# A GNN layer in one pipeline: x + beta split over two engines, two output tiles normalised by ScalarE, and the end transposes moved between the update halves

## The chip, the cores and the metric

The kernel runs on one core of a Trainium2 chip. A time is device microseconds of one execution. Its engines work side by side, each through its own instruction list in order, and meet at semaphores: TensorE (PE; its weight loads, which overlap the matmuls, are PEld), VectorE (DVE), ScalarE (ACT), GpSimd (POOL) and SyncE (SP), which here only issues DMAs.

## The reference

With 50,000 nodes of 128 features and 25,000 edges sorted by destination:

```python
h = relu(layernorm(x))                                    # no gamma, beta
e = [h[src], h[dst], edge_attr, node_vec[src], node_vec[dst]]
messages = silu(e @ mW1 + mb1) @ mW2 + mb2
agg = segment_sum(messages, dst)
u = silu([h, agg, node_vec] @ uW1 + ub1)
out = x + layernorm(h + u @ uW2 + ub2) * gamma + beta
```

All of it is float32.

## The kernel before, in words

Work is cut into 49 edge steps of 512 edges (4 tiles of 128) and 49 node steps of 1,024 nodes (8 tiles of 128). One software pipeline runs over iterations; each engine has a function `body(it)` that issues its part of iteration `it`. Iteration n handles edge step n (`new`: gathers and statistics), n-1 (`own`: normalise and transpose the gathered ends), n-2 (`e`: message network), and node steps n-3 (`nxt`), n-4 (`near`), n-5 (`k`), n-6 (`prev`). There are 56 iterations; edges end first, so the last ones are nodes alone. A first iteration is written out, then the sortedness of the edges is checked; the path used here is `WHOLE`.

What each engine does in an iteration, in order:

- **GpSimd** issues 8 indirect DMAs that gather the end rows of `new` (L373), then adds beta to the whole x tile of `near` (`x_beta`, L393, 1,024 columns).
- **TensorE**: (a) node hidden layer of `k`, L445 and L447, in which a 0/1 matrix `match` sums the messages of each node; (b) edge hidden layer of `e`, L456 to L458; (c) 8 transposes of `x_norm` of `near` into the PSUM tensor `ps_t`, L464; (d) edge output of `e`, L469; (e) the node update of `k` into `ps_upd`, 8 tiles in two halves of four, L476 and L477; each half waits until VectorE has read the same half of the step before (`centred_ready`); (f) 8 transposes of `ends_norm` of `own` into the same `ps_t`, L486, and 4 of edge features, L490. (f) waits for ScalarE's `ends_norm`. The next iteration's (a) stands behind (f).
- **ScalarE**: (1) copies `ps_t` and `ps_f` of `e` out, L537 and L538; (2) normalises 8 tiles into `x_norm`, L532; (3) silu into `hidden_n`, L549; (4) silu into `hidden_e`, L553; (5) copies the transposed x out of `ps_t` as `h_t`, L557, which waits for (c) on TensorE; (6) normalises 8 tiles into `ends_norm`, L532.
- **VectorE**: `bn_stats` of 8 tiles of `ps_upd` of `prev` (L677), 8 of x (L681), 8 of the gathered ends (L685, L686); copies the destination index (L652); then a chain of small operations on [128, 24] values that makes 1/sqrt(var) by an integer guess, a Halley and a Newton step (L702 to L743), with the eight `centred` operations (L632, `(ps_upd - mean) * gamma`) put between its links, and the message eviction (L643), `place` (L661) and `match` (L670) behind them. `rstd` and `minus` (= -mean * rstd) end the chain; then 8 operations `y_out = centred * rstd + x_beta` (L749).
- **SyncE** issues loads and stores in ring buffers of four (x, ends) or two (output, `match`).

```python
for j in range(N_TILES):
    if j % E_TILES == 0:
        wait(pe, centred_ready, 2 * k.n - 1 + j // E_TILES)
```

The order within each engine's list is written by hand; there is no planner.

## Time and profile before

| | us |
|---|---|
| median of three runs | 720.5 (715.4 to 722.17) |
| the profiled execution's own time | 722.67 |
| its span, first to last instruction | 720.8 |
| busy: TensorE / VectorE / ScalarE / GpSimd | 630.0 / 642.1 / 516.5 / 541.0 |
| mean granted TensorE clock, share of full | 0.974 |

The busy times are sums over the whole span, each of one engine; two engines near 90% do not say which of them sets the pace, since a wait of one for the other can run in a ring. A timeline row gives start, length and, in brackets, how long the engine had been idle before it and what it had waited for.

### The profile page before, as it was taken

The numbers are of one execution on the slowest core, as the hardware profiler recorded it, in microseconds if no ns is written. First come the engines' busy times: TensorE is split into PE (matmuls) and PEld (weight loads), VectorE is DVE, ScalarE is ACT, GpSimd is POOL, SyncE is SP. The second block draws the span as 40 slices with busy tenths as digits, with TensorE's granted clock in tenths as the row PEclk, the third lists the DMA queues.
The fourth block names the chain that finished last, engine by engine and source line by source line (L and its number), as shares of the span: only waits on it lengthen the run. The fifth ranks groups of instructions, "written<-read, shape, count | busy, mean of one in ns | idle before, by whom it ended". The sixth has DMA issues, their size and how long they took to land.

```text
span 720.8 us, 17511 instructions
## 1 busy us (share of the span) xinstructions
PE 630.0 (87%) x3830; PEld 466.2 (65%) x3830; DVE 642.1 (89%) x3060; ACT 516.5 (72%) x1034; POOL 541.0 (75%) x448
## 2 busy tenths in 40 slices
PE   1468999999999999999998998998998998999981
PEld 0235676766776776766766766766767767767771
DVE  4365699999999999999999999999999999999897
ACT  1546778778877787787787787787788788788630
POOL 7778878888888888888888888888888888881210
PEclk9966999999999999999999999999999999999997
DMA  6445556666666666666765766756666766765231
GB/s 133 111 115 131 151 164 160 186 187 163 180 186 163 190 179 163 189 181 161 194 177 160 204 169 166 202 163 170 199 160 179 196 156 180 198 161 173 87 122 69
DMA packets 119053, 118.54 MB, mean 164 GB/s; under 512 B 48764, under 2 KB 93615, under 8 KB 119010
## 3 DMA queue, kind: packets, MB, share of 16 engines
q1 hardware_dynamic: 104884, 91.41, 43.6%
q0 software_dynamic: 12608, 26.25, 16.4%
q10 hardware_dynamic: 1518, 0.42, 0.3%
q8 instruction: 13, 0.21, 0.1%
q14 instruction: 30, 0.25, 0.1%
HBM read 79.31 MB, written 38.70 MB: 164 GB/s over the span
## 4 chain that ended last, share of the span: by engine, by line
POOL 60%; issue 21%; PE 8%; DVE 6%; ACT 2%; DMA 1%; POOLq 1%; ACTq 0%
POOL ends_in L373 47%; POOL x_beta L393 13%; ACT ends_norm L532 2%; DVE y_out L749 1%; DVE centred L632 1%; PE ps_e L458 1%; PE ps_t L486 1%; PE ps_hid L445 1%; PE ps_hid L447 1%; PE ps_e L457 1%; PE ps_e L456 1%; DVE stats L677 1%; PE ps_t L464 1%; DMA ends_in<-in_rows,end_idx 1%; PE ps_f L490 0%
## 5 line engine op out<-in xcount | busy, mean ns | idle before, releaser
L373 POOL DMA_INDIRECT ends_in<-in_rows,end_idx x392 | 422.6, 1078 | 113.3 <-issue 112.5
L476 PE MATMUL ps_upd<-w_out,hidden_n 128*128 128x128 f32 x784 | 140.4, 284 | 33.6 <-DVE centred L632 31.6
L532 ACT ACTIVATE ends_norm<-ends_in,minus,rstd 128x128 f32<-128x128 f32 x392 | 155.9, 484 | 6.6 <-DVE minus L743 6.6
L532 ACT ACTIVATE x_norm<-x_in,minus,rstd 128x128 f32<-128x128 f32 x392 | 156.0, 488 | 6.3 <-DVE minus L743 6.3
L476 PEld LDWEIGHTS ps_upd<-w_out,hidden_n 128*128 128x128 f32 x784 | 119.4, 192 | 41.9 <-DVE centred L632 26.4
L393 POOL TENSOR_TENSOR x_beta<-x_in,beta_row 128x1024 f32<-128x1024 f32 x49 | 116.0, 2368 | 39.1 <-DVE y_out L749 38.2
L632 DVE SCALAR_TENSOR_TENSOR centred<-ps_upd,y_mean,gamma_row 128x128 f32<-128x128 f32 x392 | 135.0, 347 | 0.1
L447 PEld LDWEIGHTS ps_hid<-match,msg_in 113*128 113x128 f32 x784 | 103.0, 191 | 47.2 <-issue 47.2
L537 ACT ACTIVATE ends_t<-ps_t 128x1024 f32<-128x1024 f32 x49 | 50.2, 1024 | 90.9 <-PE ps_f L490 89.3
L477 PE MATMUL ps_upd<-const_sb,h_t 128*128 128x128 f32 x392 | 107.6, 274 | 0.0
L749 DVE SCALAR_TENSOR_TENSOR y_out<-centred,rstd,x_beta 128x128 f32<-128x128 f32 x392 | 107.1, 348 | 0.0
L447 PE MATMUL ps_hid<-match,msg_in 113*128 113x128 f32 x784 | 103.4, 275 | 0.0
L445 PE MATMUL ps_hid<-h_t,w_node 128*128 128x512 f32 x196 | 100.8, 596 | 0.1
L685 DVE BATCH_NORM_STATS2 stats<-ends_in 128x6 f32<-128x128 f32 x196 | 55.5, 283 | 48.6 <-DMA ends_in<-in_rows,end_idx 48.6
L677 DVE BATCH_NORM_STATS2 stats<-ps_upd 128x6 f32<-128x128 f32 x392 | 82.3, 287 | 0.0
L681 DVE BATCH_NORM_STATS2 stats<-x_in 128x6 f32<-128x128 f32 x392 | 80.1, 284 | 0.0
L486 PE MATMUL ps_t<-const_sb,ends_norm 128*128 128x128 f32 x392 | 54.5, 284 | 25.3 <-ACT ends_norm L532 25.2
L557 ACT ACTIVATE h_t<-ps_t,b_col 128x1024 f32<-128x1024 f32 x49 | 54.6, 1114 | 19.6 <-PE ps_t L464 15.4
L464 PEld LDWEIGHTS ps_t<-const_sb,x_norm 128*128 128x128 f32 x392 | 42.9, 143 | 36.4 <-issue 36.4
L553 ACT ACTIVATE hidden_e<-ps_e,mb_col 128x512 f32<-128x512 f32 x49 | 33.7, 688 | 43.3 <-PE ps_e L458 43.3
L486 PEld LDWEIGHTS ps_t<-const_sb,ends_norm 128*128 128x128 f32 x392 | 45.5, 146 | 29.6 <-ACT ends_norm L532 29.6
L549 ACT ACTIVATE hidden_n<-ps_hid,node_bias 128x1024 f32<-128x1024 f32 x49 | 54.2, 1107 | 8.7 <-PE ps_hid L447 8.7
(79 smaller groups left out, 885.7 us busy)
## 6 DMA issues: line engine op xcount, KB each, us to landing
x_in<-in_x_steps SPq DMA_DIRECT2D x49, 512.0 KB, 5.2
out<-y_out SPq DMA_DIRECT2D x49, 512.0 KB
msg_in<-msgs SPq DMA_DIRECT2D x392, 56.4 KB
msgs<-msg SPq DMA_DIRECT2D x49, 258.0 KB
ends_in<-in_rows,end_idx POOLq DMA_INDIRECT x392
ends_in<-in_attr SPq DMA_DIRECT2D x49, 64.0 KB
end_idx<-in_ends SPq DMA_DIRECT2D x49, 4.0 KB
match<-in_node_vec SPq DMA_DIRECT2D x49, 4.0 KB
```

Of the source, the lines that this page charges most:

```text
L373: nc.gpsimd.indirect_dma_start(out=dst, out_offset=None, in_=rows, in_offset=bass.IndirectOffsetOnAxis(ap=end_idx[s.slot][:, t, side:side ...
L393: nc.gpsimd.tensor_tensor(x_beta[near.slot][:, :, :], x_in[near.slot][:, :, :], beta_row[:, :, :].broadcast_to([P, N_TILES, H]), ALU.add). ...
L445: nc.tensor.matmul(ps_hid[:, bank], w_node[:, :], h_t[k.half][:, bank], start=True, stop=False)
L447: last = nc.tensor.matmul(ps_hid[:, cols(j)], msg_in[k.half][0:WINDOW + 1, j, 0:H], match[k.half][0:WINDOW + 1, j, :], start=False, stop=e ...
L476: nc.tensor.matmul(ps_upd[:, cols(j)], hidden_n[:, cols(j)], w_out[:, :], start=j % E_TILES == 0, stop=False)
L477: last = nc.tensor.matmul(ps_upd[:, cols(j)], h_t[k.half][:, cols(j)], ident, is_transpose=True, start=False, stop=j % E_TILES == E_TILES - 1)
L486: nc.tensor.transpose(ps_t[:, cols(t)], ends_norm[own.half][:, t, :], ident)
L532: return nc.scalar.activation(dst, source, function, bias=minus[was][:, c:c + 1], scale=rstd[was][:, c:c + 1])
L632: last = V.scalar_tensor_tensor(centred[:, j, :], ps_upd[:, j * P:(j + 1) * P], y_mean[:, j:j + 1], gamma_row[:, 0, :], ALU.subtract, ALU. ...
L677: last = V.bn_stats(stats[:, Y_AT + j, :], ps_upd[:, j * P:(j + 1) * P])
L681: last = V.bn_stats(stats[:, 2 * E_TILES + j, :], x_in[nxt.slot][:, j, :])
L749: last = V.scalar_tensor_tensor(y_out[prev.half][:, j, :], centred[:, j, :], rstd[b][:, Y_AT + j:Y_AT + j + 1], x_beta[prev.slot][:, j, :] ...
```

## The change

- `x_beta` is split: GpSimd adds beta to tiles 0 to 4, VectorE to tiles 5 to 7 (`add_beta`, between `rstd` and `minus`), with a semaphore each.
- `place` and `match` become one operation: an index row of 0 to 1,023 is loaded once by a DMA on GpSimd's queue (`iota`, 512 KB in SBUF), and `match` is `(iota + base) == destination`. It now stands behind `minus`.
- The root takes one small operation less (the factor 0.375 is carried through).
- The copy of the destination index goes from VectorE to ScalarE, ahead of `h_t`.
- Output tiles 6 and 7 are no longer centred by VectorE. ScalarE computes `y_norm = ps_upd * rstd + minus` from PSUM behind `ends_norm`, once `minus` is there; VectorE then multiplies by gamma and adds `x_beta`, two operations of 256 columns that depend on each other. `centred_ready` counts after tiles 3 and 5.
- TensorE's update is split: half 0, then the end transposes (f), then half 1, which waits for `y_norm_ready` too.

The diff, cut to its core (leading spaces cut):

```diff
...
+POOL_TILES = 5
+ACT_TILES = 2
+DVE_TILES = N_TILES - ACT_TILES
 RING = 4
...
-C_IDENT, C_LOWER, C_IOTA = 0, P, 2 * P
-C_BOUND = 3 * P
+C_IDENT, C_LOWER = 0, P
+C_BOUND = 2 * P
 C_SEARCH = C_BOUND + PER_LANE + 1
...
         wait_apart(sp, x_norm_ready, k.n - RING + 1, sp_passed)
-        wait_apart(sp, x_beta_ready, k.n - RING + 1, sp_passed)
+        wait_apart(sp, x_beta_low_ready, k.n - RING + 1, sp_passed)
+        wait_apart(sp, x_beta_high_ready, k.n - RING + 1, sp_passed)
         sp.dma_start(x_in[b][:, :, :], x_v[k.n]).then_inc(x_loaded[b], 16)
...
                 pool.wait_ge(out_ready, done.n + 1)
-            nc.gpsimd.tensor_tensor(x_beta[near.slot][:, :, :], x_in[near.slot][:, :, :],
-                                    beta_row[:, :, :].broadcast_to([P, N_TILES, H]), ALU.add).then_inc(x_beta_ready, 1)
+            nc.gpsimd.tensor_tensor(x_beta[near.slot][:, 0:POOL_TILES, :], x_in[near.slot][:, 0:POOL_TILES, :],
+                                    beta_row[:, :, :].broadcast_to([P, POOL_TILES, H]), ALU.add).then_inc(x_beta_low_ready, 1)
...
         pool.dma_start(dst, source).then_inc(late_loaded, 16)
+    pool.dma_start(iota[:, :, :].rearrange("p j m -> p (j m)"), iota_row.rearrange("(o n) -> o n", o=1).broadcast_to([P, N_STEP])).then_inc(iota_loaded, 16)
     run_steps(pool, body, scatter)
...
     pe.wait_ge(weights_loaded, 16 * N_WEIGHTS)
+
+    def update_half(k, half):
+        for j in range(half * HALF, (half + 1) * HALF):
+            nc.tensor.matmul(ps_upd[:, cols(j)], hidden_n[:, cols(j)], w_out[:, :], start=j % HALF == 0, stop=False)
+            last = nc.tensor.matmul(ps_upd[:, cols(j)], h_t[k.half][:, cols(j)], ident, is_transpose=True,
+                                    start=False, stop=j % HALF == HALF - 1)
+        last.then_inc(update_summed, 1)
...
             pe.wait_ge(hidden_n_ready, k.n + 1)
-            for j in range(N_TILES):
-                if j % E_TILES == 0:
-                    wait(pe, centred_ready, 2 * k.n - 1 + j // E_TILES)
-                nc.tensor.matmul(ps_upd[:, cols(j)], hidden_n[:, cols(j)], w_out[:, :], start=j % E_TILES == 0, stop=False)
-                last = nc.tensor.matmul(ps_upd[:, cols(j)], h_t[k.half][:, cols(j)], ident, is_transpose=True,
-                                        start=False, stop=j % E_TILES == E_TILES - 1)
-                if j % E_TILES == E_TILES - 1:
-                    last.then_inc(update_summed, 1)
+            wait(pe, centred_ready, 2 * k.n - 1)
+            update_half(k, 0)
         if own:
...
             last.then_inc(ends_transposed, 1)
+        if k:
+            wait(pe, centred_ready, 2 * k.n)
+            wait(pe, y_norm_ready, k.n)
+            update_half(k, 1)
...
             nc.scalar.activation(hidden_e[:, :], ps_e[:, :], ACT.Silu, bias=mb1_col[:, :]).then_inc(hidden_e_ready, 1)
+        if own:
+            act.wait_ge(edge_loaded[own.slot], (own.fills4 + 1) * 16)
+            wait(act, msg_stored[own.slot], 16 * own.fills4)
+            nc.scalar.activation(msg[own.slot][:, :, H:H + 1], end_idx[own.slot][:, :, 1:2], ACT.Copy).then_inc(dst_copied, 1)
         if near:
...
             last.then_inc(ends_norm_ready, 1)
+        if prev:
+            act.wait_ge(rstd_ready, 2 * it.stats_before() + 2)
+            wait(act, y_scaled, prev.n)
+            for j in range(DVE_TILES, N_TILES):
+                at = Y_AT + j
+                last = nc.scalar.activation(y_norm[:, j - DVE_TILES, :], ps_upd[:, j * P:(j + 1) * P], ACT.Identity,
+                                            bias=minus[it.phase][:, at:at + 1], scale=rstd[it.phase][:, at:at + 1])
+            last.then_inc(y_norm_ready, 1)
...
-STAT_OPS = 12
-HALF = N_TILES // 2
-Y_AT = 2 * E_TILES + N_TILES
+STAT_OPS = 11
...
     V = nc.vector
-    iota = const[:, C_IOTA:C_IOTA + P].rearrange("p (o m) -> p o m", o=1)
...
                                           ALU.subtract, ALU.mult)
-            if j % HALF == HALF - 1:
+            if j in (HALF - 1, DVE_TILES - 1):
                 last.then_inc(centred_ready, 1)
...
-        def copy_dst():
-
-            if not own:
-                return
-            dve.wait_ge(edge_loaded[own.slot], (own.fills4 + 1) * 16)
-            wait(dve, msg_stored[own.slot], 16 * own.fills4)
-            V.tensor_copy(msg[own.slot][:, :, H:H + 1], end_idx[own.slot][:, :, 1:2]).then_inc(dst_copied, 1)
-
-        def place_messages():
+        def match_nodes():
...
                 dve.wait_ge(msg_loaded[near.half], 16 * N_TILES * (near.fills2 + 1))
-            base = const[0:WINDOW, bass.ds(C_BASE + N_TILES * near.n, N_TILES)].rearrange("p (j o) -> p j o", o=1)
-            V.tensor_tensor(place[near.half][0:WINDOW, :, :], msg_in[near.half][0:WINDOW, :, H:H + 1],
-                            base, ALU.subtract).then_inc(place_ready, 1)
-
-        def match_nodes():
+            wait(dve, hidden_n_summed, near.n - 1)
+            if isinstance(near.n, int) and near.n == 0:
+                dve.wait_ge(iota_loaded, 16)
+            V.scalar_tensor_tensor(match[near.half][0:WINDOW, :, :], iota[0:WINDOW, :, :],
+                                   const[0:WINDOW, bass.ds(C_BASE + N_TILES * near.n, 1)],
+                                   msg_in[near.half][0:WINDOW, :, H:H + 1].broadcast_to([WINDOW, N_TILES, P]),
+                                   ALU.add, ALU.is_equal).then_inc(match_ready, 1)
+
+        def add_beta():
...
                 return
-            dve.wait_ge(place_ready, near.n + 1)
-            wait(dve, hidden_n_summed, near.n - 1)
-            V.tensor_tensor(match[near.half][0:WINDOW, :, :], place[near.half][0:WINDOW, :, :].broadcast_to([WINDOW, N_TILES, P]),
-                            iota[0:WINDOW, :, :].broadcast_to([WINDOW, N_TILES, P]), ALU.is_equal).then_inc(match_ready, 1)
+            wait(dve, out_ready, near.n - RING + 1)
+            if isinstance(near.n, int) and near.n == 0:
+                dve.wait_ge(late_loaded, 16 * N_LATE)
+            V.tensor_tensor(x_beta[near.slot][:, POOL_TILES:, :], x_in[near.slot][:, POOL_TILES:, :],
+                            beta_row[:, :, :].broadcast_to([P, N_TILES - POOL_TILES, H]), ALU.add).then_inc(x_beta_high_ready, 1)
...
         dve.wait_ge(stat_ops, base + 7)
-        V.tensor_scalar(root_c[:, at], root_b[:, at], 0.375, -1.25, ALU.mult, ALU.add).then_inc(stat_ops, 1)
+        V.scalar_tensor_tensor(root_c[:, at], root_b[:, at], 10.0 / 3.0, root_b[:, at], ALU.subtract, ALU.mult).then_inc(stat_ops, 1)
         centre(5)
         dve.wait_ge(stat_ops, base + 8)
-        V.tensor_tensor(root_d[:, at], root_c[:, at], root_b[:, at], ALU.mult).then_inc(stat_ops, 1)
-        centre(6)
+        V.scalar_tensor_tensor(halley[:, at], root_c[:, at], 5.0, guess[:, at], ALU.add, ALU.mult).then_inc(stat_ops, 1)
         dve.wait_ge(stat_ops, base + 9)
-        V.scalar_tensor_tensor(halley[:, at], root_d[:, at], 1.875, guess[:, at], ALU.add, ALU.mult).then_inc(stat_ops, 1)
-        centre(7)
+        V.tensor_tensor(newton_a[:, at], halley[:, at], halley[:, at], ALU.mult).then_inc(stat_ops, 1)
         dve.wait_ge(stat_ops, base + 10)
-        V.tensor_tensor(newton_a[:, at], halley[:, at], halley[:, at], ALU.mult).then_inc(stat_ops, 1)
+        V.scalar_tensor_tensor(newton_b[:, at], newton_a[:, at], -0.5 * 0.375 ** 3, var[:, at], ALU.mult, ALU.mult).then_inc(stat_ops, 1)
         evict_messages()
         dve.wait_ge(stat_ops, base + 11)
-        V.scalar_tensor_tensor(newton_b[:, at], newton_a[:, at], -0.5, var[:, at], ALU.mult, ALU.mult).then_inc(stat_ops, 1)
-        place_messages()
-        dve.wait_ge(stat_ops, base + 12)
         wait(dve, ends_norm_ready, it.edges_upto(-RING))
         wait(dve, x_norm_ready, it.nodes_upto(-2))
-        V.scalar_tensor_tensor(rstd[b][:, at], newton_b[:, at], 1.5, halley[:, at], ALU.add, ALU.mult).then_inc(rstd_ready, 1)
-        match_nodes()
+        V.scalar_tensor_tensor(rstd[b][:, at], newton_b[:, at], 1.5 * 0.375, halley[:, at], ALU.add, ALU.mult).then_inc(rstd_ready, 1)
+        add_beta()
         dve.wait_ge(rstd_ready, 2 * it.stats_before() + 1)
         V.scalar_tensor_tensor(minus[b][:, at], s_add[:, at], -0.5, rstd[b][:, at], ALU.mult, ALU.mult).then_inc(rstd_ready, 1)
+        match_nodes()
         if prev:
             dve.wait_ge(centred_ready, 2 * prev.n + 2)
-            dve.wait_ge(x_beta_ready, prev.n + 1)
+            dve.wait_ge(x_beta_low_ready, prev.n + 1)
+            dve.wait_ge(x_beta_high_ready, prev.n + 1)
             wait(dve, stored[prev.half], 16 * prev.fills2)
-            for j in range(N_TILES):
-                last = V.scalar_tensor_tensor(y_out[prev.half][:, j, :], centred[:, j, :], rstd[b][:, Y_AT + j:Y_AT + j + 1],
-                                              x_beta[prev.slot][:, j, :], ALU.mult, ALU.add)
-            last.then_inc(out_ready, 1)
+            for j in range(DVE_TILES):
+                V.scalar_tensor_tensor(y_out[prev.half][:, j, :], centred[:, j, :], rstd[b][:, Y_AT + j:Y_AT + j + 1],
+                                       x_beta[prev.slot][:, j, :], ALU.mult, ALU.add)
+            dve.wait_ge(y_norm_ready, prev.n + 1)
+            V.tensor_tensor(centred[:, DVE_TILES:, :], y_norm[:, :, :], gamma_row[:, :, :].broadcast_to([P, ACT_TILES, H]),
+                            ALU.mult).then_inc(y_scaled, 1)
+            dve.wait_ge(y_scaled, prev.n + 1)
+            V.tensor_tensor(y_out[prev.half][:, DVE_TILES:, :], centred[:, DVE_TILES:, :], x_beta[prev.slot][:, DVE_TILES:, :],
+                            ALU.add).then_inc(out_ready, 1)
...
```

## Rows read from the trace of the kernel before

**Rows 1.** The page: busy time by engine; chain that ended last; one transfer's landing time.
```profile
PE 630.0 (87%) x3830; PEld 466.2 (65%) x3830; DVE 642.1 (89%) x3060; ACT 516.5 (72%) x1034; POOL 541.0 (75%) x448
...
POOL 60%; issue 21%; PE 8%; DVE 6%; ACT 2%; DMA 1%; POOLq 1%; ACTq 0%
...
x_in<-in_x_steps SPq DMA_DIRECT2D x49, 512.0 KB, 5.2
```

**Rows 2.** Stretches: start:end and length, busy by engine, PEclk, DMA share, GB/s.
```profile
76.66:89.78 13.12, 12.41 (x80) 9.22 (x79) 10.66 (x53) 10.46 (x23) 10.81 (x10) 1.00 0.52 129
...
89.78:102.89 13.11, 12.40 (x80) 9.20 (x79) 12.59 (x61) 10.45 (x22) 9.66 (x8) 1.00 0.58 157
...
663.73:720.80 57.07, 37.75 (x249) 30.66 (x247) 49.72 (x237) 22.31 (x43) 7.07 (x3) 0.88 0.32 103
...
76.66:663.73 587.07, 550.23 (x3434) 409.29 (x3433) 553.77 (x2625) 460.44 (x925) 474.62 (x382) 1.00 0.64 175
```

**Rows 3.** Timeline of two early iterations: start, length, engine, instruction, idle before it.
```profile
79.89 1.09 PE L486 MATMUL ps_t<-const_sb,ends_norm 128*128 128x128 f32 x8 [0.71 <-ACT ends_norm L532]
...
88.76 1.11 ACT L557 ACTIVATE h_t<-ps_t,b_col 128x1024 f32<-128x1024 f32 x1 [0.34 <-PE ps_t L464]
...
89.47 0.39 PE L476 MATMUL ps_upd<-w_out,hidden_n 128*128 128x128 f32 x2
...
89.78 3.18 ACT L532 ACTIVATE ends_norm<-ends_in,minus,rstd 128x128 f32<-128x128 f32 x8
...
91.80 0.39 PE L476 MATMUL ps_upd<-w_out,hidden_n 128*128 128x128 f32 x2
...
93.01 1.09 PE L486 MATMUL ps_t<-const_sb,ends_norm 128*128 128x128 f32 x8 [0.71 <-ACT ends_norm L532]
```

**Rows 4.** Timeline of the last iteration that transposes edge ends, ScalarE.
```profile
663.73 3.19 ACT L532 ACTIVATE ends_norm<-ends_in,minus,rstd 128x128 f32<-128x128 f32 x8
```

**Rows 5.** Timeline of one iteration of the long middle stretch.
```profile
414.01 1.90 POOL L373 DMA_INDIRECT ends_in<-in_rows,end_idx  x1 [0.31 <-issue]
...
418.85 0.29 DVE L685 BATCH_NORM_STATS2 stats<-ends_in 128x6 f32<-128x128 f32 x1 [0.62 <-DMA ends_in<-in_rows,end_idx]
...
422.66 0.49 PE L476 MATMUL ps_upd<-w_out,hidden_n 128*128 128x128 f32 x2 [0.78 <-DVE centred L632]
```

**Rows 6.** Groups by line and shape: count, busy us, mean ns, idle before.
```profile
L409 POOL DMA_DIRECT2D gamma_row<-in_gamma x1 | 0.7, 726 | 0.0
...
L393 POOL TENSOR_TENSOR x_beta<-x_in,beta_row 128x1024 f32<-128x1024 f32 x49 | 116.0, 2368 | 39.1 <-DVE y_out L749 38.2
...
L661 DVE TENSOR_TENSOR place<-msg_in,const_sb 112x8 f32<-112x8 f32 x49 | 9.0, 184 | 0.0
...
L632 DVE SCALAR_TENSOR_TENSOR centred<-ps_upd,y_mean,gamma_row 128x128 f32<-128x128 f32 x392 | 135.0, 347 | 0.1
...
L749 DVE SCALAR_TENSOR_TENSOR y_out<-centred,rstd,x_beta 128x128 f32<-128x128 f32 x392 | 107.1, 348 | 0.0
...
L670 DVE TENSOR_TENSOR match<-place,const_sb 112x1024 f32<-112x1024 f32 x49 | 59.9, 1223 | 0.0
...
L532 ACT ACTIVATE x_norm<-x_in,minus,rstd 128x128 f32<-128x128 f32 x392 | 156.0, 488 | 6.3 <-DVE minus L743 6.3
```

**Rows 7.** Timeline of TensorE: four pauses, in the fill and in the tail.
```profile
36.36 1.09 PE L486 MATMUL ps_t<-const_sb,ends_norm 128*128 128x128 f32 x8 [1.92 <-ACT ends_norm L532]
...
40.18 1.10 PE L456 MATMUL ps_e<-ends_t,w_src 128*128 128x512 f32 x2 [2.29 <-DVE msg L643]
...
686.38 0.77 PE L476 MATMUL ps_upd<-w_out,hidden_n 128*128 128x128 f32 x2 [2.62 <-DVE centred L632]
...
704.54 0.46 PE L476 MATMUL ps_upd<-w_out,hidden_n 128*128 128x128 f32 x2 [1.99 <-DVE centred L632]
```

**Rows 8.** Stretches of two microseconds behind the third of these pauses.
```profile
687.00:689.00 2.00, 2.00 (x11) 2.00 (x10) 1.97 (x8) 0.00 (x0) 0.00 (x0) 0.50 0.61 244
...
689.00:691.00 2.00, 2.00 (x15) 1.93 (x14) 2.00 (x9) 1.65 (x5) 0.00 (x0) 0.81 0.00 0
```

27 lines of the change are left out of this document (13 added, 14 removed).

## The prediction

> **What bounds the kernel now.** The page comes first. TensorE (630.0 us) and VectorE (642.1) are both busy for nearly 90% of the span, and the chain that ended last runs for 60% over GpSimd [rows 1]. That names three candidates and settles nothing, so the iteration itself has to be read. The reader should look for the stretch where one ring of waits runs alone, and then for what is added to it later.
>
> The two iterations from 76.66 to 102.89 take 13.12 and 13.11 us [rows 2]. In them GpSimd is well ahead, and TensorE's one idle time is 0.71 us in front of the end transposes (f), waiting for ScalarE's `ends_norm` [rows 3]. This is a ring over two engines. Followed in the rows: (f) starts at 79.89; behind it TensorE runs (a), (b), (c) without a gap; 8.87 us later, at 88.76, ScalarE can copy `h_t`; `ends_norm` follows at 89.78 and lasts 3.18; at 93.01 the next (f) starts. 93.01 - 79.89 = 13.12 [rows 3]. While ScalarE does `h_t` and `ends_norm` (4.2 us), TensorE does (d) and all of the update (e): that is what fills the pause but for 0.71.
>
> Later the mean is a little longer. `ends_norm` of the 5th edge step starts at 76.66, 13.12 ahead of the one at 89.78, and that of the 49th at 663.73 [rows 2 to 4], so 587.07 / 44 = 13.34 us [rows 2]. The 0.22 above the ring is GpSimd's: it has no idle time beyond its issue gaps, one gather per iteration is stretched to 1.90 us, VectorE waits 0.62 for the gathered ends, is thereby late with `centred`, and TensorE's wait (0.78) now stands in front of the update [rows 5]. So three rings lie close together: GpSimd 13.34, TensorE with ScalarE 13.12, VectorE 13.34 - 0.62 = 12.7.
>
> **The change, part by part.** Sums are made against the profiled execution: span 720.8, time 722.67, which is 2.2 above the median of the three runs.
>
> *x + beta split.* GpSimd's 2.37 us [rows 6] falls to five eighths, 1.48: its ring goes from 13.34 to about 12.45. Alone that is worth at most the 0.22 down to the next ring.
>
> *VectorE.* Removed: the index copy and `place` (0.18 each, by the row of `place`), one small link (0.18), two `centred` (0.69) and two `y_out` (0.70) [rows 6], in all 1.93. Added: `add_beta`, 384 columns, and two operations of 256 columns. By the row of `match` (1,024 columns in 1.22) they are 0.46 + 0.31 + 0.31 = 1.1; with a fixed part as large as a whole 0.18 each, 1.6. Three links of the chain lose the `centred` operation that covered their latency, and the last addition waits for the multiplication before it: about 0.1 to 0.15 each, 0.5. The fused `match` I take at its old 1.22. VectorE's own ring stays at 12.7 - 1.9 + 1.6 to 2.1 = 12.4 to 12.9. It is not the bound, whatever the exact price.
>
> *ScalarE.* The index copy goes in front of `h_t`, where ScalarE idles 0.34 [rows 3]. The shortest row of a like kind is 0.18, on VectorE; the 0.488 of an `x_norm` tile [rows 6] is an upper end. I take 0, since the idle time hides it; the upper end would add 0.15 to the ring, 6.6 us in all. `y_norm` is two tiles of at most 0.488, 0.9 us, behind `ends_norm`, where ScalarE has been waiting for (f) anyway. `minus` is there earlier than before relative to VectorE's work, as `match` now stands behind it.
>
> *The transposes between the halves.* This is the step that counts. Behind VectorE's `centred`, half 0 can still run while ScalarE does `ends_norm`. Half 1 can't: it stands behind (f) on TensorE's list, (f) waits for `ends_norm`, and the next (a) stands behind half 1. `y_norm` (0.9) ends before (f) does (1.4), so that new wait costs nothing, but the four tiles of half 1 move from the pause into the ring. Their price: seven tiles start between 89.47 and 91.80 [rows 3], 0.333 each, so 1.33. What is queued behind: (a), (b), (c), `h_t` and `ends_norm`, thus the whole of the next iteration. The ring becomes 13.12 + 1.33 = 14.45, and the pause in front of (f) becomes 0.71 + 1.33 = 2.04. All other rings (12.45, 12.4 to 12.9) fit in it. VectorE's next wait is for the edge output (d), about 1.2 us an iteration, and costs nothing.
>
> Half 1 of 44 iterations lies between the 5th and the 49th `ends_norm`: 44 x (14.45 - 13.34) = +48.8. The half behind the last one adds 1.33 to the tail.
>
> *The tail* is 57.07 us from there [rows 2], paced by VectorE. Half 1 must there wait for `minus` and `y_norm`, then VectorE for half 1; against that, `match` no longer stands in front of `minus`. Followed iteration by iteration the `minus` times come within 1 us of the old ones plus the 1.33; I take 0 more, with -2 and +5 as ends.
>
> *The start.* One more DMA issue on GpSimd, 0.73 by the row of gamma's [rows 6], stands in front of nothing but the gathers, for which VectorE waits; its 512 KB share the way with them, at most the 5.2 us that as large an x tile takes [rows 1]. I take +1, nearer to the issue, since the wait at the start is for the last gather.
>
> Sum: 48.8 + 1.3 + 0 + 1 = +51. Execution 722.67 + 51 = 774; against the median, 772. I say **773**.
>
> **A rule that speaks against the change.** TensorE's granted clock stayed at its upper level (2.4 GHz) across pauses of 1.92 and 1.99 us, and fell to the lower (1.2 GHz) soon after pauses of 2.29 and 2.62 [rows 7]; behind the pause that ended at 686.38 it was low until about 689.8, since 0.81 in the second of two stretches is 0.76 us at 0.50 and the rest at 1.00 [rows 8]. The change makes a pause of 2.04 in every iteration. The Trainium skill, page "TensorE: Matmul & The Clock Gate", section "HAM oscillation — how this bites in real kernels", describes a kernel whose TensorE waited between groups of matmuls and so began each group at the low clock. [...]
>
> **The rivals.**
>
> *The clock falls, too.* A low stretch of 3.4 us loses 1.7 us of work, all of it in the ring, since (f), half 1 and (a) are what follows. In every iteration: 44 x 1.7 = +75, 848 us. For it: the pauses that ended in a fall are only 0.25 longer. Against: 2.04 is nearer to 1.99, and the pause is the only one of the iteration. If it happens, then I expect it in a part of the iterations; at two in five, 30 us more: 803. Chance 0.2.
>
> *Half 1 costs nothing, the result is a little faster.* In the middle stretch the trace shows TensorE idle in front of the update, not in front of (f) [rows 5]. If the end transposes have to wait for VectorE's lateness there, and the change removes that lateness, TensorE could take half 1 in the time it gets back. Place: between the update and (f). It decides only if `ends_norm` is ready by the time half 0 ends, 2.04 us earlier than the early rows allow. Then the period falls to the 13.12 of [rows 3], and 44 x 0.22 = 10 less the start's 1 gives 713. Against: ScalarE's list puts `ends_norm` behind `h_t`, so it can't come earlier. Chance 0.05; that would also be the outcome if the order of TensorE's list were not what the diff says.
>
> *Something between*: part of the 1.33 is absorbed, or the split's gain and the loss nearly meet, 714 to 762. Chance 0.07, of which 0.03 lies within 1% of before.
>
> **How the numbers follow.** Forecast 0.68 with its own range 762 to 785 (the bounds of start, tail and ScalarE's copy); clock rival 0.2, from 785 up; the faster rival 0.05; between 0.07. The range of 8 in 10 is 762 to 806: it takes in the forecast and most of the clock rival. About 1%, 7 us, is what a measurement of this kernel can tell from no change, given runs from 715.4 to 722.17. Faster by over 1%: 0.05; within: 0.03; slower: 0.92.
>
> **What would show it.** Right, if the `ends_norm` groups stand 14.4 to 14.5 us apart in the middle, TensorE's idle time before L486 is about 2.0 and that before the update is gone, GpSimd and VectorE show waits of over 1 us per iteration (GpSimd for its ring buffers, VectorE for L469 in front of the eviction), and the granted clock of the middle is 1.00. The clock rival would show there as 0.9 or less, with L445 at twice its time in some iterations. Wrong, if the groups stand under 13.5 apart, or if TensorE waits for `y_norm` in front of half 1, which would mean that `minus` comes after `ends_norm` and the period is VectorE's.

## The result, and the profile after

| | before | after |
|---|---|---|
| median, us | 720.1 (715.4 to 722.17) | 810.9 (809.19 to 811.33) |
| ratio after / before | | 1.127 [1.121, 1.132] |
| span of the profiled execution | 720.8 | 809.0 |
| mean granted clock | 0.974 | 0.942 |

The change made the kernel 12.7% slower. The forecast was 773, range 762 to 806: the direction and the longer ring were right, the time was 38 us too low and outside the range, since the clock fell as well.

The page of the changed kernel: busy time by engine, granted clock in 40 slices, the chain that ended last, and two groups by line (count, busy us, mean ns, idle before and what ended it).

```profile
PE 660.5 (82%) x3830; PEld 495.1 (61%) x3830; DVE 655.3 (81%) x2858; ACT 559.9 (69%) x1181; POOL 454.3 (56%) x449
...
PEclk9979999999999999999999999999999999999997
...
PE 65%; ACT 18%; issue 8%; DVE 5%; POOL 1%; ACTq 1%; DMA 0%; DVEq 0%; POOLq 0%
...
L399 POOL TENSOR_TENSOR x_beta<-x_in,beta_row 128x640 f32<-128x640 f32 x49 | 75.8, 1546 | 211.8 <-DVE y_out L768 211.6
...
L494 PE MATMUL ps_t<-const_sb,ends_norm 128*128 128x128 f32 x392 | 58.2, 295 | 111.4 <-ACT ends_norm L544 111.4
```

The chain has left GpSimd (60% in [rows 1]) and runs over TensorE and ScalarE. GpSimd now waits 4.6 us an iteration (211.6 over 46 waits). TensorE's instructions are as many as before, 3,830, but 30.5 us more busy: the same work at a lower clock. The slices show no slice of the middle below 0.9, which hides where the low clock lies; that needs stretches.

Stretches of the changed kernel, with the columns of [rows 2]: four iterations one by one, each from one start of `ends_norm` to the next; three short stretches inside the third; then the middle and the tail that answer to those of [rows 2].

```profile
91.84:106.28 14.44, 12.41 (x80) 9.21 (x79) 12.84 (x57) 11.35 (x26) 7.50 (x8) 1.00 0.49 135
106.28:120.80 14.52, 12.48 (x81) 9.29 (x80) 12.89 (x57) 11.35 (x25) 9.32 (x10) 1.00 0.52 134
120.80:136.97 16.17, 14.05 (x81) 10.86 (x80) 13.08 (x57) 11.35 (x26) 10.67 (x11) 0.89 0.66 186
136.97:151.49 14.52, 12.40 (x81) 9.21 (x80) 12.94 (x57) 11.35 (x26) 7.81 (x9) 1.00 0.51 138
...
124.00:126.00 2.00, 1.97 (x12) 1.98 (x13) 1.97 (x9) 0.67 (x2) 0.28 (x1) 0.68 0.41 133
126.00:128.00 2.00, 2.00 (x12) 2.00 (x11) 0.43 (x3) 1.72 (x3) 1.86 (x2) 0.50 0.15 30
128.00:130.00 2.00, 2.00 (x13) 1.52 (x13) 1.43 (x8) 2.00 (x7) 1.39 (x3) 0.97 0.58 128
...
77.40:748.68 671.28, 578.75 (x3434) 437.84 (x3433) 567.41 (x2449) 498.65 (x1056) 389.74 (x380) 0.95 0.56 154
748.68:809.00 60.32, 38.51 (x249) 30.75 (x247) 49.88 (x221) 26.86 (x55) 4.62 (x3) 0.90 0.27 87
```

An iteration takes 14.44 or 14.52 us, or 1.65 more. In the longer ones the granted clock falls behind the pause of TensorE to its lower level (1.2 of 2.4 GHz): 0.68, 0.50 and 0.97 in three stretches of 2 us are 1.28, 2.00 and 0.12 us at half, 3.4 us in all, which lose 1.7 us of work.

The starts of `ends_norm` in the middle's 44 iterations give the count. From the 3rd to the 38th iteration they alternate strictly, 14.52, 16.17, 14.52, and so on, 18 of each; among the last six there are two more falls, which makes 20. The first two and the last six, which are written out and lie outside the hardware loop, take 14.44 (16.09 with a fall), those inside it 14.52: 8 x 14.44 + 36 x 14.52 + 20 x 1.65 = 671.2, the 671.28 of the row.

So the time went here: middle 671.28 - 587.07 = +84.2, tail 60.32 - 57.07 = +3.2, start 77.40 - 76.66 = +0.7, together the 88.2 between the spans. Of the 84.2, 20 x 1.65 = 33 are the clock, and 51 the longer ring.

The timeline of the changed kernel, two iterations of the fill and one of the loop, with the columns of [rows 3].

```profile
80.63 1.09 PE L494 MATMUL ps_t<-const_sb,ends_norm 128*128 128x128 f32 x8 [2.04 <-ACT ends_norm L544]
...
90.39 0.20 ACT L569 ACTIVATE msg<-end_idx 128x4 f32<-128x4 int32 x1
...
90.83 1.11 ACT L573 ACTIVATE h_t<-ps_t,b_col 128x1024 f32<-128x1024 f32 x1 [0.24 <-PE ps_t L478]
...
91.84 3.17 ACT L544 ACTIVATE ends_norm<-ends_in,minus,rstd 128x128 f32<-128x128 f32 x8
...
94.92 0.79 ACT L587 ACTIVATE y_norm<-ps_upd,minus,rstd 128x128 f32<-128x128 f32 x2
...
95.07 1.09 PE L494 MATMUL ps_t<-const_sb,ends_norm 128*128 128x128 f32 x8 [2.03 <-ACT ends_norm L544]
...
96.43 0.39 PE L440 MATMUL ps_upd<-w_out,hidden_n 128*128 128x128 f32 x2
...
124.03 1.36 PE L494 MATMUL ps_t<-const_sb,ends_norm 128*128 128x128 f32 x8 [2.12 <-ACT ends_norm L544]
```

The pause in front of (f) was 0.71 in [rows 3] and is 2.04 now, 2.12 inside the loop. From one (f) to the next, 95.07 - 80.63 = 14.44, against 13.12. Half 1 begins at 96.43, behind (f); TensorE does it while nothing else of the ring can go on. At 124.03 the eight transposes take 1.36 in place of 1.09: the clock falls within them.

Waits of the changed kernel: us in total, times, longest.

```profile
DVE stats L695 <- PE ps_upd L441: 57.3, 45, 2.2
DVE msg L664 <- PE ps_e L483: 50.8, 47, 5.3
...
PE ps_upd L440 <- ACT y_norm L587: 4.2, 4, 1.2
```

VectorE now waits for TensorE at two places, over 1 us at each. Half 1 waited for `y_norm` four times in all: the new wait is not what costs.

### The profile page after: what moved, and what is told of

Its sections match the earlier page's. It is cut to its first block, busy times and chain, and to the rows that moved or that the text cites. A ratio compares the mean times of both kernels' runs of the same rounds, so it can differ in the third digit from the quotient of the medians.

```text
span 809.0 us, 17646 instructions
## 1 busy us (share of the span) xinstructions
PE 660.5 (82%) x3830; PEld 495.1 (61%) x3830; DVE 655.3 (81%) x2858; ACT 559.9 (69%) x1181; POOL 454.3 (56%) x449
## 4 chain that ended last, share of the span: by engine, by line
PE 65%; ACT 18%; issue 8%; DVE 5%; POOL 1%; ACTq 1%; DMA 0%; DVEq 0%; POOLq 0%
ACT ends_norm L544 18%; PE ps_hid L461 10%; PE ps_hid L459 10%; PE ps_t L494 7%; PE ps_upd L440 7%; PE ps_e L472 7%; PE ps_t L478 6%; PE ps_e L470 6%; PE ps_e L471 6%; PE ps_f L498 4%; PE ps_upd L441 3%; DVE y_out L762 1%; POOL ends_in L379 1%; DVE centred L653 1%; DVE stats L695 1%
## 5 line engine op out<-in xcount | busy, mean ns | idle before, releaser
L379 POOL DMA_INDIRECT ends_in<-in_rows,end_idx x392 | 375.6, 958 | 115.3 <-issue 110.8
L399 POOL TENSOR_TENSOR x_beta<-x_in,beta_row 128x640 f32<-128x640 f32 x49 | 75.8, 1546 | 211.8 <-DVE y_out L768 211.6
L440 PE MATMUL ps_upd<-w_out,hidden_n 128*128 128x128 f32 x784 | 159.6, 306 | 7.7 <-ACT y_norm L587 4.2
L494 PE MATMUL ps_t<-const_sb,ends_norm 128*128 128x128 f32 x392 | 58.2, 295 | 111.4 <-ACT ends_norm L544 111.4
L440 PEld LDWEIGHTS ps_upd<-w_out,hidden_n 128*128 128x128 f32 x784 | 139.0, 222 | 9.1 <-issue 7.2
L695 DVE BATCH_NORM_STATS2 stats<-ps_upd 128x6 f32<-128x128 f32 x392 | 86.6, 284 | 58.1 <-PE ps_upd L441 57.3
L441 PE MATMUL ps_upd<-const_sb,h_t 128*128 128x128 f32 x392 | 117.8, 301 | 0.0
L653 DVE SCALAR_TENSOR_TENSOR centred<-ps_upd,y_mean,gamma_row 128x128 f32<-128x128 f32 x294 | 100.8, 344 | 0.4
L762 DVE SCALAR_TENSOR_TENSOR y_out<-centred,rstd,x_beta 128x128 f32<-128x128 f32 x294 | 81.2, 344 | 0.0
L664 DVE TENSOR_TENSOR msg<-ps_e,fold_bias 128x512 f32<-128x512 f32 x49 | 33.9, 691 | 50.8 <-PE ps_e L483 50.8
```

The source lines that it names most:

```text
L379: nc.gpsimd.indirect_dma_start(out=dst, out_offset=None, in_=rows, in_offset=bass.IndirectOffsetOnAxis(ap=end_idx[s.slot][:, t, side:side ...
L399: nc.gpsimd.tensor_tensor(x_beta[near.slot][:, 0:POOL_TILES, :], x_in[near.slot][:, 0:POOL_TILES, :], beta_row[:, :, :].broadcast_to([P, P ...
L440: nc.tensor.matmul(ps_upd[:, cols(j)], hidden_n[:, cols(j)], w_out[:, :], start=j % HALF == 0, stop=False)
L441: last = nc.tensor.matmul(ps_upd[:, cols(j)], h_t[k.half][:, cols(j)], ident, is_transpose=True, start=False, stop=j % HALF == HALF - 1)
L494: nc.tensor.transpose(ps_t[:, cols(t)], ends_norm[own.half][:, t, :], ident)
L653: last = V.scalar_tensor_tensor(centred[:, j, :], ps_upd[:, j * P:(j + 1) * P], y_mean[:, j:j + 1], gamma_row[:, 0, :], ALU.subtract, ALU. ...
```

## The experiments

The first four ran on one chip, where the kernel before took 722.26 us (718.9 to 724.14); the last two on another, where it took 721.78 (719.42 to 724.88).

**1. The order alone.** The kernel before, with nothing of the change but the second update half behind the end transposes.

```diff
                     pe.wait_ge(hidden_n_ready, k.n + 1)
-                    for j in range(N_TILES):
+                    for j in range(0 * E_TILES, 1 * E_TILES):
...
                     last.then_inc(ends_transposed, 1)
+                if k:
+                    for j in range(1 * E_TILES, 2 * E_TILES):
...
```

> The kernel before with one edit: the second half of TensorE's update stands behind the end transposes. x + beta, match, the root and the output tiles are as before. Theory (the four tiles moved into the ring of TensorE and ScalarE, 14.45 us, and the pause of 2.04 us that they leave is followed by a low clock in about every second iteration, 1.65 us each): 795 to 812 us, ends_norm groups 14.4 or 16.1 apart, clock 0.93 to 0.95. Rival (the loss comes with y_norm, its wait or VectorE's new operations): within 2% of before, 706 to 735. Second rival (the ring is right but the clock needs the new work too): 765 to 780 with the clock at 1.00 in the middle.

Measured: 808.82 us (808.22 to 809.63), ratio 1.120 [1.117, 1.123]. Its stretches:

```profile
105.34:119.86 14.52, 12.48 (x81) 9.29 (x80) 12.75 (x61) 10.56 (x22) 10.79 (x10) 1.00 0.60 150
119.86:136.03 16.17, 14.06 (x81) 10.86 (x80) 12.76 (x61) 10.56 (x22) 12.13 (x11) 0.89 0.61 161
76.46:747.74 671.28, 578.73 (x3434) 437.65 (x3433) 556.39 (x2625) 464.85 (x925) 441.59 (x383) 0.95 0.56 154
```

The middle lasts 671.28 us, to the hundredth what it lasts in the changed kernel, with the same alternation and again 20 falls. The moved half carries the whole loss. Everything else in the change, `y_norm`, VectorE's new operations, the lighter GpSimd, is off the path as long as that half is in it.

**2. The pause filled.** The changed kernel, with two thrown-away matmuls of 512 columns into `ps_f` between half 0 and the wait for `ends_norm`. They add work and take nothing away.

```diff
                 if own:
+                    wait(pe, ends_copied, own.n)
+                    if k:
+                        nc.tensor.matmul(ps_f[:, 0:512], w_out[:, :], hidden_n[:, 0:512], start=True, stop=True)
+                        nc.tensor.matmul(ps_f[:, 0:512], w_out[:, :], hidden_n[:, 0:512], start=True, stop=True)
                     pe.wait_ge(ends_norm_ready, own.n + 1)
-                    wait(pe, ends_copied, own.n)
```

> The changed kernel with two matmuls of 128x512 float32 on TensorE between the first half of the update and the wait for ends_norm; their result is thrown away (they write the PSUM bank that the feature transposes then overwrite). They take 1.7 us, less than the pause of 2.04. Theory (the clock falls because of the pause): the clock stays at its upper level in the middle, every iteration takes 14.45, and the time is 768 to 780 us, 35 us less than the changed kernel though TensorE does more work. Rival (the alternate long iterations have another cause, such as transfers or the order of semaphores): 805 us or more, since work is only added.

Measured: 775.18 us (774.66 to 776.15), ratio 1.074 [1.071, 1.077]; with more work 36 us less than the changed kernel, and 34 less than experiment 1 on the same chip. Its stretches, one iteration and the whole middle:

```profile
105.12:119.65 14.53, 14.21 (x85) 9.95 (x84) 12.91 (x57) 11.37 (x26) 9.30 (x10) 1.00 0.59 145
...
76.25:714.56 638.31, 621.38 (x3610) 433.85 (x3609) 567.87 (x2449) 498.99 (x1055) 398.42 (x381) 1.00 0.60 162
```

Its timeline, TensorE in front of (f):

```profile
135.12 1.02 PE L492 MATMUL ps_f<-hidden_n,w_out 128*128 128x512 f32 x2
135.98 1.02 PE L493 MATMUL ps_f<-hidden_n,w_out 128*128 128x512 f32 x2
137.40 1.09 PE L497 MATMUL ps_t<-const_sb,ends_norm 128*128 128x128 f32 x8 [0.40 <-ACT ends_norm L547]
```

With 0.40 us left of the pause, all 44 iterations take 14.44 to 14.53 and the clock of the middle is 1.00. 671.28 - 638.31 = 33.0 us is thus the price of the falls, and 638.31 - 587.07 = 51.2 that of the moved half against the kernel before, whose middle was itself 0.22 an iteration above its ring. This is the kernel that the forecast of 773 described: the ring as forecast, the clock up.

**3. Both halves ahead again, but waiting for `y_norm`.** The changed kernel with half 1 back in front of (f) and with its waits. It moves the same four tiles into the ring and adds `y_norm` to it.

```diff
             update_half(k, 0)
+            wait(pe, centred_ready, 2 * k.n)
+            wait(pe, y_norm_ready, k.n)
+            update_half(k, 1)
...
-        if k:
-            wait(pe, centred_ready, 2 * k.n)
-            wait(pe, y_norm_ready, k.n)
-            update_half(k, 1)
```

> The changed kernel with the second half of the update moved back ahead of the end transposes, still waiting for y_norm. Theory (ScalarE's y_norm follows ends_norm, so the ring then holds ends_norm, y_norm 0.7, half 1 1.33 and the transposes): 15.15 us an iteration at the high clock, 804 us; the pause grows to about 2.8, and with a low stretch behind each one it is up to 16.8 an iteration, 875 us. So 804 to 880, slower than the changed kernel: its order is the better one of the two once y_norm is there. Rival (the order of transposes and halves is the whole loss, y_norm costs nothing): 711 to 725.

Measured: 877.52 us (877.07 to 879.25), ratio 1.216 [1.212, 1.220]. One iteration as a stretch, then its timeline:

```profile
139.14:156.12 16.98, 14.08 (x81) 10.91 (x80) 13.04 (x57) 11.24 (x26) 9.10 (x9) 0.90 0.52 142
```

```profile
139.14 3.18 ACT L543 ACTIVATE ends_norm<-ends_in,minus,rstd 128x128 f32<-128x128 f32 x8
...
142.22 0.79 ACT L586 ACTIVATE y_norm<-ps_upd,minus,rstd 128x128 f32<-128x128 f32 x2
...
143.16 0.66 PE L440 MATMUL ps_upd<-w_out,hidden_n 128*128 128x128 f32 x2 [2.90 <-ACT y_norm L586]
```

The ring is 13.12 + 0.79 (`y_norm`) + 1.33 (half 1) = 15.24, and one iteration outside the loop takes exactly that. 41 of the 44 show the fall as well (of the other three, the first has no `y_norm` yet and takes 13.12), and 16.98 is the usual length. The first matmul pair behind the pause of 2.90 takes 0.66 in place of 0.39. So with `y_norm` behind `ends_norm` on ScalarE, half 1 behind (f) is 67 us better than half 1 in front of it. Whether another place of `y_norm` in ScalarE's list would leave room for both halves ahead of (f) was not tried.

**4. The rest of the change alone.** The changed kernel without the two scalar tiles (`ACT_TILES = 0`, `y_norm` and its two operations gone, eight `centred` and eight `y_out` as before) and with both halves ahead of (f). It keeps the split of `x_beta`, the fused `match`, the shorter root and ScalarE's copy.

```diff
-ACT_TILES = 2
+ACT_TILES = 0
...
             update_half(k, 0)
+            wait(pe, centred_ready, 2 * k.n)
+            update_half(k, 1)
...
-            if prev:
-                act.wait_ge(rstd_ready, 2 * it.stats_before() + 2)
...
-                last.then_inc(y_norm_ready, 1)
```

> The changed kernel without its two last parts: all eight output tiles are VectorE's again, and both halves of the update stand ahead of the end transposes. The x + beta split, the fused match, the shorter root and ScalarE's index copy stay. Theory: the ring is 13.12 us again and nothing else is as long (GpSimd 12.45, VectorE 12.7), so 705 to 715 us, 44 x 0.22 less than before. Rival (the small parts carry some of the loss, by VectorE's added operations or by ScalarE's copy in front of h_t): 725 or more.

Measured: 734.38 us (733.63 to 734.55), ratio 1.017 [1.014, 1.019]. That is 1.7% slower than before, where 705 to 715 us was expected. GpSimd has 0.8 us less to do per iteration, and the iteration is longer, 13.63 against 13.34. The middle as a stretch:

```profile
75.19:675.08 599.89, 550.39 (x3434) 409.98 (x3433) 563.68 (x2537) 464.00 (x969) 484.46 (x383) 1.00 0.65 172
```

The timeline of GpSimd and VectorE there, one iteration:

```profile
404.83 3.07 POOL L379 DMA_INDIRECT ends_in<-in_rows,end_idx  x1 [0.30 <-issue]
...
404.91 2.18 DVE L754 SCALAR_TENSOR_TENSOR y_out<-centred,rstd,x_beta 128x128 f32<-128x128 f32 x8
...
408.21 0.94 POOL L379 DMA_INDIRECT ends_in<-in_rows,end_idx  x1 [0.30 <-issue]
...
409.16 1.56 POOL L399 TENSOR_TENSOR x_beta<-x_in,beta_row 128x640 f32<-128x640 f32 x1
...
410.88 0.30 DVE L693 BATCH_NORM_STATS2 stats<-ends_in 128x6 f32<-128x128 f32 x1 [0.66 <-DMA ends_in<-in_rows,end_idx]
...
418.41 3.09 POOL L379 DMA_INDIRECT ends_in<-in_rows,end_idx  x1 [0.30 <-issue]
418.49 2.19 DVE L754 SCALAR_TENSOR_TENSOR y_out<-centred,rstd,x_beta 128x128 f32<-128x128 f32 x8
```

And two rows of the same place in the kernel before, beside those of [rows 5]:

```profile
405.57 0.30 DVE L685 BATCH_NORM_STATS2 stats<-ends_in 128x6 f32<-128x128 f32 x1 [0.63 <-DMA ends_in<-in_rows,end_idx]
...
412.90 2.18 DVE L749 SCALAR_TENSOR_TENSOR y_out<-centred,rstd,x_beta 128x128 f32<-128x128 f32 x8
```

A gather takes 0.94 us. The one issued 0.08 ahead of `y_out` takes 3.07 and ends at 407.90, 0.81 behind the end of `y_out` (404.91 + 2.18 = 407.09). In the kernel before, the gather of [rows 5] starts at 414.01, in the middle of `y_out`, takes 1.90 and ends at 415.91, 0.83 behind the end of `y_out` (415.08). So the start of such a gather doesn't matter; its end is set by VectorE. Time that GpSimd saves ahead of it becomes a longer hold.

What sets the period is then a ring over VectorE and GpSimd: last gather landed, VectorE's path from the first edge statistics to `y_out`, the eight `y_out`, the rest of the held gather, one more gather, its landing. In the kernel before it adds up to the iteration: 7.33 + 2.18 + 0.83 + 2.94 (from the gather's end at 415.91 to 418.85) = 13.28. In these rows the path has changed: 418.49 - 410.88 = 7.61 us against 412.90 - 405.57 = 7.33, since `add_beta` stands in it and `match` is 1.28 in place of 1.22. Over 25 iterations in the loop, the path has a mean of 7.65 against 7.41, and what follows the held gather 3.12 against 3.00; the hold beyond `y_out` is 0.82 in both. So most of the 0.29 between the two periods stands in VectorE's path. This is read from the two traces; the run that was to test it is among those not answered.

The Trainium skill, page "SBUF — State Buffer", section "Who interferes with whom", says that an instruction of VectorE with two inputs in SBUF, as `y_out` has, contends with a GpSimd instruction that reads SBUF, because its second input comes through a read interface that the two engines share. A gather reads its indices in SBUF (`end_idx` in its rows), but the page does not name indirect DMAs there, and the same section reports a probe in which `tensor_tensor` on VectorE did not stall a DMA. The trace agrees as far as the gather ends only behind VectorE's work, and it shows a gather held across all eight instructions, not until the end of the first. That the port is the cause is not shown by any run here.

**5. The held gather let through.** Experiment 4, with seven of the eight x statistics of the next node step (one input each) taken from behind `y_out` and put between its eight operations. No work is added or removed.

```diff
                 if nxt:
-                    dve.wait_ge(x_loaded[nxt.slot], 16 * (nxt.fills4 + 1))
-                    for j in range(N_TILES):
-                        last = V.bn_stats(stats[:, 2 * E_TILES + j, :], x_in[nxt.slot][:, j, :])
+                    last = x_stats(nxt, N_TILES - 1)
...
                     last = V.scalar_tensor_tensor(y_out[prev.half][:, j, :], centred[:, j, :], rstd[b][:, Y_AT + j:Y_AT + j + 1],
                                                   x_beta[prev.slot][:, j, :], ALU.mult, ALU.add)
+                    if ahead and j < N_TILES - 1:
+                        x_stats(ahead, j)
```

> The kernel of e8_out_between_stats once more, on a chip where before takes its 720 us. If a run of VectorE operations with two SBUF inputs holds a gather until its end, one-input statistics between them let it through: stretched gather under 1.5 us in place of 3.1, 708 to 718 us against 734 of e2_no_scalar_tiles. If not, 730 or more.

Measured: 716.84 us (714.39 to 721.34, 8 runs), ratio 0.994 [0.991, 0.997]. The middle as a stretch, and the timeline:

```profile
76.25:656.24 579.99, 545.92 (x3434) 405.33 (x3433) 566.72 (x2537) 464.01 (x969) 415.85 (x381) 1.00 0.67 178
```

```profile
406.84 1.38 POOL L379 DMA_INDIRECT ends_in<-in_rows,end_idx  x1 [0.30 <-issue]
...
408.52 1.24 POOL L379 DMA_INDIRECT ends_in<-in_rows,end_idx  x1 [0.30 <-issue]
408.60 0.34 DVE L761 SCALAR_TENSOR_TENSOR y_out<-centred,rstd,x_beta 128x128 f32<-128x128 f32 x1
...
409.07 0.33 DVE L761 SCALAR_TENSOR_TENSOR y_out<-centred,rstd,x_beta 128x128 f32<-128x128 f32 x1
```

The gather issued 0.08 ahead of `y_out` takes 1.24 in place of 3.07. It ends at 409.76, 0.82 behind the first `y_out` (408.60 + 0.34). GpSimd's busy time in the middle falls by 68.6 us with all but the same instructions, 383 and 381 (484.46 to 415.85), and the middle by 19.9, to 13.18 an iteration, the TensorE ring of [rows 3] with the loop's 0.08. That the hold was a term of experiment 4's period is thereby shown. It does not show by itself where the loss against the kernel before came from, which has a hold too.

**6. The TensorE ring shortened too.** Experiment 5, with ScalarE's `ends_norm` put ahead of `h_t`.

```diff
+            if own:
+                act.wait_ge(rstd_ready, 2 * it.stats_before())
...
             if near:
                 act.wait_ge(x_transposed, near.n + 1)
...
-            if own:
-                act.wait_ge(rstd_ready, 2 * it.stats_before())
...
```

> The kernel of e9_both once more: the gathers let through, and ends_norm ahead of h_t on ScalarE, which takes 0.45 us out of the ring of 13.2. 690 to 703 us if the ring is what the rows say; as g8_out_between_stats if another wait takes its place.

Measured: 715.08 us (714.05 to 717.15), ratio 0.990 [0.986, 0.994]: a gain, but far from what was expected. Its first six iterations of the middle and the other 38 as stretches, then its timeline:

```profile
74.75:151.81 77.06, 74.41 (x470) 55.31 (x469) 73.53 (x320) 62.60 (x135) 54.70 (x52) 1.00 0.62 163
151.81:657.06 505.25, 475.92 (x2966) 354.60 (x2965) 490.49 (x2210) 396.45 (x838) 363.47 (x332) 1.00 0.67 178
```

```profile
408.07 1.27 DVE L672 SCALAR_TENSOR_TENSOR match<-iota_sb,const_sb,msg_in 112x1024 f32<-112x1024 f32 x1
...
408.41 2.01 POOL L379 DMA_INDIRECT ends_in<-in_rows,end_idx  x1 [0.30 <-issue]
...
409.26 0.34 DVE L761 SCALAR_TENSOR_TENSOR y_out<-centred,rstd,x_beta 128x128 f32<-128x128 f32 x1
```

The ring is shorter, 77.06 / 6 = 12.84, and TensorE has no pause left. Later the mean is 505.25 / 38 = 13.30. There a gather that starts into `match` is held over it and the first `y_out` behind it (2.01 us, ending 0.82 behind 409.60), and the period is again that of VectorE and GpSimd: VectorE is busy for 490.49 / 38 = 12.91 of the 13.30. Both this and experiment 5 beat the changed kernel, and by 1.0% and 0.6% the kernel before; the two can't be told from each other by these intervals.

**Not answered.** Four more questions were tried, on chips where the kernel before itself took 1033 to 1044 us, with its engines standing still for several us at a time inside the hardware loop; what was measured there can't be set against the other runs.

| edit | us | ratio to before there |
|---|---|---|
| changed kernel, one thrown-away matmul of 256 columns in the pause | 1050.45, 1054.17, 1062.35 | 1.014, 1.022, 1.024 |
| experiment 4 with all of `x_beta` on GpSimd | 1025.46, 1031.62, 1047.02 | 0.992, 0.996, 1.003 |
| experiment 5 | 1023.7, 1020.3 | -, 0.983 |
| experiment 6 | 987.28, 989.46 | 0.950, 0.951 |
| experiment 6 with `match` in two halves, a statistic behind each | 1005.82 | 0.969 [0.957, 0.980] |
| kernel before, with only the two reorderings of experiments 5 and 6 | 1018.76 | 0.983 [0.970, 0.996] |

The first was to say whether a pause of 1.6 us keeps the clock up; it was tried on three occasions:

> The changed kernel with one thrown-away matmul of 128x256 float32 in TensorE's pause, 0.43 us, so that 1.6 us are left of 2.04. Theory (the clock falls by the length of the pause, and pauses up to 2.0 were seen without a fall): the clock stays up, 768 to 780 us as with the pause filled. Rival (a filled pause is needed altogether): a fall in some iterations, 785 to 811.

> The kernel of e3b_pause_filled_little again, for the same reason: a pause of 1.6 us left. If the clock goes by the length of the pause it stays up, 768 to 780 us; if the pause has to be filled altogether, 785 to 811.

> The kernel of e3b_pause_filled_little, on a chip where before takes its 720 us: a pause of 1.6 us is left of 2.04. If the clock goes by the length of the pause it stays up, 768 to 780 us; if the pause has to be filled altogether, 785 to 811.

The last two times that (f) runs, behind the hardware loop, the engines don't stand still on any of the three occasions. The pause in front of it is 1.60 there, and the granted clock stays at 1.00 behind each of these six pauses. That points to the first answer and doesn't settle it, since the changed kernel too has a fall in only two of its last six.

The second was to tell VectorE's path from GpSimd's load as the cause of experiment 4's loss:

> The kernel of e2_no_scalar_tiles with the x + beta addition back on GpSimd as a whole: GpSimd gets 0.8 us more per iteration, VectorE 0.45 us less. New theory, from the trace of e2_no_scalar_tiles: a gather issued while y_out runs ends only 0.9 us after y_out does, so the ring is gathers landed, VectorE's path to the end of y_out, the rest of that gather, one more gather, landing; GpSimd's own load is not in it and VectorE's path is. Then this kernel is faster than e2_no_scalar_tiles by 44 x 0.4, 713 to 722 us, though the engine with the longer chain of work gets more of it. Rival (GpSimd's load sets the pace, as the prediction had it): 750 us or more; or no difference.

> The kernel of e7_beta_all_gpsimd again, since on the chip of that call every kernel, the one before too, took over 980 us with ScalarE standing still for several us at a time. Expectation as there: if GpSimd's gather is held until y_out ends, VectorE's path counts and GpSimd's own load doesn't, and this is 44 x 0.4 us faster than e2_no_scalar_tiles (734): 713 to 722. If GpSimd's load sets the pace, 750 or more.

> The kernel of e2_no_scalar_tiles with the x + beta addition back on GpSimd as a whole, on a chip where before takes its 720 us. GpSimd gets 0.8 us more an iteration, VectorE 0.45 less. If a gather issued into y_out is held until y_out ends, the period is gathers landed, VectorE's path to the end of y_out, and the rest of two gathers: then it falls by 0.4 from 13.7, 713 to 722 us against 734. If GpSimd's load sets the pace, 750 or more; if VectorE's path doesn't count, 734.

The kernels of experiments 5 and 6, ahead of the runs told above:

> The kernel of e2_no_scalar_tiles with one reorder on VectorE: seven of the eight x statistics of the next iteration (one SBUF input each) are put between the eight y_out operations (two SBUF inputs each) instead of standing after them. Work is the same. Theory (a run of two-input operations holds GpSimd's gather up until its end): the stretched gather of 3.1 us shrinks to under 1.5, the period falls from 13.7 to TensorE and ScalarE's 13.2, 708 to 718 us. Rival (a gather is held as long as VectorE has such work at all, or the stretch has another cause): 730 us or more, and longer out_ready.

> The kernel of e8_out_between_stats again, for the same reason. If a run of VectorE operations with two SBUF inputs holds a gather until its end, one-input statistics between them let it through: stretched gather under 1.5 us in place of 3.1, 708 to 718 us. If not, 730 or more.

> As e8_out_between_stats, and ScalarE's ends_norm moved ahead of h_t, so that it no longer waits for the x transposes. Theory: the ring of TensorE and ScalarE gets shorter by the time between hidden_e and h_t, 0.45 us, to 12.75; VectorE's own 12.7 to 12.9 is then the longest. 690 to 703 us, faster than both kernels. Rival (the ring isn't what the rows say, or another wait takes its place at once): as e8_out_between_stats.

> The kernel of e9_both again, for the same reason: the gathers let through, and ends_norm ahead of h_t on ScalarE, which takes 0.45 us out of the ring. 690 to 703 us if the ring is what the rows say; as f8_out_between_stats if another wait takes its place.

The last two were to say whether the gain of experiments 5 and 6 can be had in full, and without the change:

> The kernel of g9_both with match in two halves of four tiles, an x statistic behind each. In the trace of g9 the first six iterations took the 12.82 of the shortened ring, later ones 13.0 to 13.7 with a gather of 2.0 us that had started into match and the first y_out. Theory (a gather waits for the end of a run of two-input operations): the longest run is now 0.65 us, the period 12.85 to 13.05, 698 to 708 us. Rival (the gathers are only held elsewhere, or VectorE's added fixed cost of some 0.1 us counts in full): 712 to 718 as g9.

> The kernel before with only the two reorders: seven x statistics between the y_out operations on VectorE, and ends_norm ahead of h_t on ScalarE. No part of the change is in it. Theory: GpSimd's own ring of gathers 10.04, addition 2.53 and what is left of the holding, 12.9 to 13.1, TensorE and ScalarE 12.82, VectorE 12.9: 700 to 712 us, faster than both kernels. Rival (the change's smaller parts are needed for it): 716 or more.

None of these is settled. Experiment 6 gained more there (5%) than on the undisturbed chip (1.0%); why is not known.

## Why the prediction was wrong, and where it was right

- **The ring of 14.45** was right. It was measured at 14.44, with the pause at 2.04 as forecast. Experiment 1 shows that the reorder alone makes it, experiment 2 that it costs 51.2 us against the 48.8 of the sum. The 2.4 between them is the loop: an iteration inside it takes 0.08 more than one written out, 36 times, 2.9 us.
- **The tail** (+1.3, with ends at -2 and +5 around it) came to +3.2, **the start** (+1) to +0.7.
- **The clock is the step that failed.** The forecast took the pause of 2.04 to be on the safe side, because "2.04 is nearer to 1.99" and the pause is the only one of an iteration, and gave the fall a chance of 0.2, and then in two of five iterations (803 us). It came in 20 of 44, at 1.65 each, 33.0 us in all, as experiment 2 shows by taking only the pause away. With a two in five share the rival's size was nearly right (30 us), and its chance far too low. The 33.0 with the 2.4 above and the 1.9 by which the tail was under, less 0.3 at the start, make 37 of the 38 us that the forecast lacked. Reading one side of a gap between 1.99 and 2.29 as a boundary was the error: those were single pauses in the fill and the tail, the new one recurs every 14.5 us. The nearest row said nothing on a pause that repeats; whether its length or its recurrence brings the fall is not told apart by these runs. The Trainium skill, page "TensorE: Matmul & The Clock Gate", section "HAM oscillation — how this bites in real kernels", describes a kernel that began each group of matmuls at the low clock behind DMA waits of about 3 to 5 us. The pauses here are shorter, and the clock fell behind every second of those of 2.04 to 2.12 and, with the 2.90 of experiment 3, behind nearly every one.
- **"its ring goes from 13.34 to about 12.45"**, said of GpSimd, failed as well, hidden in the changed kernel by the longer ring (GpSimd waits 4.6 us there). Experiment 4 brought it out: 13.63. The 1.90 us of the stretched gather was read as a part of GpSimd's own work, where it is a wait for VectorE. The row's end (415.91) lies 0.83 behind that of `y_out`, which the forecast did not look up.
- **The 0.22 above the ring** was put down to that as a whole; the hardware loop adds 0.08 to 36 of the 44 iterations, 0.07 of the 0.22. In the kernel before, the first two of the 44 iterations take 13.12, the next 13 about 13.20, and only then come 13.3 to 13.6.
- **VectorE's prices** were at the upper end: `add_beta` 0.55 (0.46 by columns), the 256-column operations 0.42 and 0.43 (0.31 each), `match` 1.28. Its busy time is 12.84 to 13.08 an iteration, where 12.4 to 12.9 was forecast, and it cost nothing in 14.44.
- **ScalarE's copy** takes 0.20 and lies in its idle time (0.24 are left of 0.34): cost 0, as forecast. **`y_norm`** takes 0.79 for two tiles and ends at 95.71, ahead of the end of (f): no wait, as forecast.
- **The faster rival** (713) fell with experiment 1: the pause in front of (f) is ScalarE's, and (f) can't start earlier.

## What to carry to other kernels

An engine's pause in a ring is where work is hidden; moving work from it to behind the wait that ends it costs its full length in every iteration, and makes the pause longer by as much. Where such a pause recurs and nears the lengths after which a trace shows TensorE's clock falling, give the fall a price of its own and a chance of about a half (20 of 44 here), and remember that thrown-away matmuls in the pause can buy it back. Before an engine is relieved of work, look at what sets the end of its longest instruction: where that lies at a fixed distance behind another engine's work, relief only lengthens the wait, and the order on the other engine is what to change.

## What the runs showed of the hardware

- A pause of 2.04 to 2.12 us in each iteration of 14.5, with TensorE busy for the rest, was followed by 3.4 us at 1.2 GHz in every second iteration, very regularly (18 times in 36 in the loop), and in 2 of the last 6. Pauses of 1.92 and 1.99 [rows 7] and of 0.40 were not. Why every second, is open.
- An indirect DMA issued by GpSimd takes 0.94 us; issued just before eight VectorE operations with two inputs in SBUF it takes 3.07, issued in their middle 1.90, and ends 0.8 us behind the last in both cases. With an operation of one input between each two it takes 1.24, and ends 0.8 us behind the first of them.
- An iteration inside the hardware loop takes 0.08 us longer than one written out, in both kernels (13.20 and 13.12; 14.52 and 14.44).
